# Wr loaded by GpSimd, product 7 by output tile, and B turned by VectorE instead of TensorE, in a two-layer fp32 kernel

## The reference

```python
# layer 0: dense W (1024x1024) plus a gated low-rank part, E=8 experts of rank R=16
base   = einsum('btd,od->bto', x, W)
logits = einsum('btd,ed->bte', x, Wr) + 5.0 * one_hot(language_id)      # Wr: 8x1024
topw, topi = top_k(logits, 2);  gates = one-hot sum of softmax(topw)
h      = einsum('btd,erd->bter', x, A)                                  # A: 8x16x1024
x = x + base + 2.0 * einsum('bter,bte,eor->bto', h, gates, B)           # B: 8x1024x16
# layer 1: one of 16 weight matrices for each batch row
x = x + einsum('bsi,boi->bso', x, w1[adapter_id])
```

## Time and profile before

| | |
|---|---|
| median of 3 runs | 396.96 us (396.77 to 397.57) |
| profiled execution | 396.9 us, of which 395.1 us are the span from the first to the last instruction |
| granted TensorE clock | 1.00 over the span (2.4 GHz, the upper of its two levels) |
| PE (TensorE matmul) busy | 389.8 us, 99% |
| DVE (VectorE) busy | 307.9 us, 78% |
| ACT (ScalarE) busy | 173.8 us, 44% |
| POOL (GpSimd) busy | 60.7 us, 15% |
| read and written in HBM | 53.51 MB and 14.68 MB |

### The profile page before, as it was taken

The page is one execution under the profiler, slowest core; times in us unless marked ns, Lnnn a source line. Parts: engine busy times, 40 slices in busy tenths (PEclk is TensorE's granted clock), DMA queues, the critical chain, the costliest instruction groups (busy, mean ns, idle before and its releaser), DMA issues.

```text
span 395.1 us, 5948 instructions
## 1 busy us (share of the span) xinstructions
PE 389.8 (99%) x1888; PEld 329.9 (83%) x1888; DVE 307.9 (78%) x415; ACT 173.8 (44%) x245; POOL 60.7 (15%) x86
## 2 busy tenths in 40 slices
PE   8999999999999999999999999999999999999996
PEld 8888988888889888888888888888888888888886
DVE  3899998988554757048877967999999999999600
ACT  3362283554400243254275334555665656556411
POOL 3134300000000000000110211332321231312000
PEclk9999999999999999999999999999999999999999
DMA  7999750113776100009492999999999999897212
GB/s 202 226 224 216 109 147 2 53 55 107 234 217 165 25 1 0 2 1 247 130 330 71 274 265 273 274 253 278 259 280 291 286 267 302 256 268 166 80 53 55
DMA packets 88129, 68.60 MB, mean 174 GB/s; under 512 B 16386, under 2 KB 87074, under 8 KB 87586
## 3 DMA queue, kind: packets, MB, share of 16 engines
q1 hardware_dynamic: 61472, 46.59, 49.2%
q10 hardware_dynamic: 26626, 21.64, 17.9%
HBM read 53.51 MB, written 14.68 MB: 173 GB/s over the span
## 4 chain that ended last, share of the span: by engine, by line
PE 97%; DMA 1%; SPq 1%; issue 0%; DVE 0%; ACT 0%
PE banks L1421 15%; PE banks L1419 15%; PE banks L1420 15%; PE banks L1282 13%; PE banks L1284 13%; PE banks L1283 13%; PE banks L1275 6%; PE banks L1260 2%; PE banks L1296 2%; PE banks L1293 2%; PE banks L1295 2%; DMA sums<-in_L_cond_Wr_dram 1%; PE banks L1314 0%; SPq L436 0%; SPq L483 0%; SPq L429 0%
## 5 line engine op out<-in xcount | busy, mean ns | idle before, releaser
L1282 PE MATMUL banks<-ring,weights 128*128 128x512 f32 x192 | 75.2, 392 | 0.0
L1420 PE MATMUL banks<-weights,tokens 128*128 128x512 f32 (+1 forms) x184 | 69.9, 380 | 0.0
L1421 PE MATMUL banks<-weights,tokens 128*128 128x512 f32 (+1 forms) x184 | 69.9, 380 | 0.0
L1419 PE MATMUL banks<-weights,tokens 128*128 128x512 f32 (+1 forms) x184 | 69.9, 380 | 0.0
L1106 ACT ACTIVATE weights<-weights_f 128x1024 fp32r<-128x1024 f32 x44 | 46.6, 1061 | 50.1 <-DVE weights_f L759 49.3
L512 POOL TENSOR_TENSOR raw<-raw,ident 128x128 f32<-128x128 f32 x42 | 30.0, 714 | 219.2 <-DMA raw<-in_L_cond_weight_dram 219.1
L759 DVE STREAM_TRANSPOSE weights_f<-raw 128x1024 f32<-128x1024 f32 x42 | 51.7, 1232 | 8.2 <-POOL raw L512 7.7
L765 DVE TENSOR_TENSOR weights<-weights_f,weights 128x1024 fp32r<-128x1024 f32 x44 | 52.7, 1198 | 0.7 <-ACT weights L1106 0.6
L1284 PE MATMUL banks<-ring,turned_w 128*128 128x512 f32 x128 | 49.8, 389 | 0.0
L1283 PE MATMUL banks<-tokens,weights 128*128 128x512 f32 x128 | 49.8, 389 | 0.0
L1282 PEld LDWEIGHTS banks<-ring,weights 128*128 128x128 f32 x192 | 36.0, 188 | 7.6 <-issue 0.3
(11 more groups left out here) (131 smaller groups left out, 626.0 us busy)
## 6 DMA issues: line engine op xcount, KB each, us to landing
raw<-in_L_cond_weight_dram SPq DMA_DIRECT2D x168, 128.0 KB, 5.2
ring_f<-in_L_cond_weight_dram SPq DMA_DIRECT2D x88, 128.0 KB, 5.5
out_dram<-sums ACTq DMA_DIRECT2D x31, 256.0 KB, 5.6
raw<-in_x_dram SPq DMA_DIRECT2D x48, 128.0 KB, 3.3
x_kept<-stage ACTq DMA_DIRECT2D x24, 256.0 KB, 3.1
raw<-in_L_cond_W_dram SPq DMA_DIRECT2D x16, 128.0 KB, 3.4
turned_w_f<-in_x_dram SPq DMA_DIRECT2D x12, 128.0 KB, 3.4
ring_f<-in_L_cond_W_dram SPq DMA_DIRECT2D x12, 128.0 KB, 3.6
```

The costliest lines, as they stand in the source:

```text
L1282: nc.tensor.matmul(ps, u_hi, x_hi, start=first and k == 0, stop=False, skip_group_check=True)
L1419: nc.tensor.matmul(ps, x_hi, w_hi, start=m == 0, stop=False)
L1420: nc.tensor.matmul(ps, x_hi, w_lo, start=False, stop=False)
L1421: mm = nc.tensor.matmul(ps, x_lo, w_hi, start=False, stop=m == M - 1)
```

## The change

1. **Front.** The four loads of Wr move from SP to GpSimd, behind the making of the identity. SP goes on from A's first half to W. A's second half moves behind the first two second halves of x, for SP and VectorE. On VectorE the low part `("wr", 0)` moves ahead of the turn of x's tile (0, 1, 0), and the bias work moves a little.
2. **Product 7 of span 0** is taken by output tile. TensorE waits for each tile's low weights and copied accumulator separately. The gated h is turned before tile 3 (36 matmuls of the product are done then, as before). Tile 3's s4, low weights and accumulator copy move behind the gates.
3. **B** is loaded so that a 32x32 block turn is all that it needs. VectorE turns it in one instruction between product 7's x parts and the gates. The 8 transposes of TensorE and the 4 copies of ScalarE go.

```diff
     def by_tile(s, i):
-        return s == 0 and i in (1, 2, 6, 5)
+        return s == 0 and i in (1, 2, 6, 7, 5)
...
@@ SyncE
             fill_a_half(sp, 0, (0, 1))
-            sp.wait_ge(wr_zeroed, 1)
-            for c in range(Q):
-                sp.dma_start(wr_raw[c * S:c * S + E, :], wr[:, c * DQ:(c + 1) * DQ]).then_inc(wr_loaded, 16)
             fill_w_half(sp, 0)
             for r in range(1, HM):
                 fill(sp, W0_PLACES[r], w0_rows(r), w_loaded[r])
+            fill_x(sp, 0, 1)
             fill_a_half(sp, 1)
-            fill_x(sp, 0, 1)
             fill_x(sp, 1, 1)
...
@@ GpSimd
+            pool.wait_ge(wr_zeroed, 1)
+            for c in range(Q):
+                pool.dma_start(wr_raw[c * S:c * S + E, :], wr[:, c * DQ:(c + 1) * DQ]).then_inc(wr_loaded, 16)
             pool.wait_ge(consts, 3)
...
@@ VectorE, the front
-            turn_half(("ah", 1))
             low(("wl", 3))
             turn_half(("xh", 0, 1))
             turn_half(("xh", 1, 1))
             low(("xr", 0))
             low(("xr", 1))
+            turn_half(("ah", 1))
             turn_half(("xh", 2, 1))
             turn_half(("xh", 3, 1))
             low(("xr", 2))
+            turn_half(("wh", 0, 1))
+            low(("xr", 3))
...
+            low(("wr", 0))
+            turn(x_item(0, 1, 0))
...
-            turn_half(("wh", 0, 1))
-            turn(x_item(0, 1, 0))
-            low(("wr", 0))
...
@@ VectorE, product 7 to the gates
-            for r in range(HM):
+            for r in range(HM - 1):
                 make_s4(r)
-            lows("u", 7)
+                low(("u", 7, r))
             lows("x", 0, 7)
+            dve.wait_ge(b_loaded, E * 16)
+            nc.vector.transpose(b_whole.rearrange("p (m q s) -> p q m s", m=M, q=Q),
+                                raw_tile(SLOT["b",]).rearrange("p (q m j) -> p q m j", q=Q, m=M)).then_inc(b_turned, 1)
             make_gates(0)
+            make_s4(HM - 1)
+            low(("u", 7, HM - 1))
             low(("b",))
             make_s1(0)
             low(("x", 0, 5, 0))
...
@@ TensorE
-                    if r == 1:
-                        turn_b()
+
+            def product_7():
+                for r in range(HM):
+                    if r == HM - 1:
+                        turn_gated(0)
+                    pe.wait_ge(lo_done, LOW_AT["u", 7, r] + 1)
+                    pe.wait_ge(u2_copied, r + 1)
+                    for k in range(HM):
+                        if r == 0:
+                            pe.wait_ge(lo_done, LOW_AT["x", 0, 7, k] + 1)
+                        step(0, 7, k, r, main_bank(0, r), False)
```

More of the change, by code:

```diff
@@ L75, in cond_resid_kernel @@
     FRONT = ([("xh", t, 0) for t in range(XT)] + [("ah", 0), ("wh", 0, 0)] + [("w", r) for r in range(1, HM)] +
-             [("ah", 1)] + [("xh", t, 1) for t in range(XT)] + [("wh", 0, 1)])
+             [("xh", 0, 1), ("xh", 1, 1), ("ah", 1), ("xh", 2, 1), ("xh", 3, 1), ("wh", 0, 1)])
     LOADS = ([x_item(0, 1, t) for t in range(XT)] + [("w", m) for m in range(HM, M)] + [("b",)] +
@@ L101, in cond_resid_kernel @@
     PIECES += [("x", 0, 6, t) for t in range(XT)] + [("u", 6, r) for r in range(HM)]
-    PIECES += [("u", 7, r) for r in range(HM)] + [("x", 0, 7, k) for k in range(HM)] + [("b",)]
+    PIECES += [("u", 7, r) for r in range(HM - 1)] + [("x", 0, 7, k) for k in range(HM)] + [("u", 7, HM - 1), ("b",)]
     PIECES += [("x", 0, 5, 0), ("u", 5, 0)] + [("x", 0, 5, k) for k in range(1, HM)] + [("u", 5, r) for r in range(1, HM)]
@@ L128, in cond_resid_kernel @@
     w1_rows = w1.rearrange("n o i -> (n o) i")
-    b_rows = b.rearrange("e (p j) r -> e p j r", p=P)
+    b_rows = b.rearrange("e (n s) r -> e s n r", s=S)
     x1_kept = nc.dram_tensor("x1_kept", [NB, P, M, T], F32, kind="Internal").ap()
@@ L279, in gT_ps @@
             return banks[:, at:at + 2, :]
-        def b_ps():
-            return banks[:, 4:6, :]
         def kept_slot(e):
@@ L326, in cond_resid_kernel @@
         b_turned = sem("b_turned")
-        b_copied = sem("b_copied")
         hi_done = sem("hi_done")
@@ L460, in load @@
                     for e in range(E):
-                        sp.dma_start(raw_tile(slot).rearrange("p (j e r) -> p e j r", j=M, e=E)[:, e],
+                        sp.dma_start(raw_tile(slot)[e // 2 * S:(e // 2 + 1) * S, :]
+                                     .rearrange("p (n i r) -> p i n r", i=2, r=R)[:, e % 2],
                                      b_rows[e]).then_inc(b_loaded, 16)
@@ L800, in _ @@
                                     lang_f[:].unsqueeze(2).to_broadcast([P, NB, E]), ALU.is_equal).then_inc(setup, 1)
-            low(("xr", 3))
+            low(("wr", 0))
+            turn(x_item(0, 1, 0))
             dve.wait_ge(setup, 3)
             nc.vector.tensor_scalar(bias[:], bias[:], LANG_BIAS, None, ALU.mult).then_inc(setup, 1)
-            turn_half(("wh", 0, 1))
-            turn(x_item(0, 1, 0))
-            low(("wr", 0))
             turn(x_item(0, 1, 1))
@@ L966, in high @@
                 elif kind == "b":
-                    act.wait_ge(b_copied, Q)
+                    act.wait_ge(b_turned, 1)
                 elif kind == "bd":
@@ L1153, in _ @@
             copy_h(0, 1)
-            highs("u", 7)
-            act.wait_ge(b_turned, 1)
-            for q in range(Q):
-                nc.scalar.activation(b_whole.rearrange("p (m q h j) -> p q m h j", m=M, q=Q, h=4)[:, q],
-                                     b_ps().rearrange("p a f -> p (a f)")
-                                     .rearrange("p (j q m h) -> p q m h j", j=M, q=Q, m=M)[:, q],
-                                     ACT.Copy).then_inc(b_copied, 1)
+            for r in range(HM - 1):
+                high(("u", 7, r))
             for r in range(HM - 1):
@@ L1163, in _ @@
             highs("x", 0, 7)
-            copy_u2(0, 3)
+            high(("u", 7, HM - 1))
             high(("b",))
@@ L1167, in _ @@
             high(("x", 0, 5, 0))
+            copy_u2(0, HM - 1)
             gT_high(0)
@@ L1297, in lora @@
                                  skip_group_check=True).then_inc(lora_done, 1)
-            def turn_b():
-                pe.wait_ge(b_loaded, E * 16)
-                pe.wait_ge(h_copied, 2)
-                flat = raw_tile(SLOT["b",])
-                for j in range(M):
-                    turn_j = nc.tensor.transpose(b_ps()[:, j // HM, (j % HM) * P:(j % HM + 1) * P],
-                                                 flat[:, j * P:(j + 1) * P], ident[:])
-                turn_j.then_inc(b_turned, 1)
             def turn_gated(s):
@@ L1310, in turn_gated @@
                 pe.wait_ge(p1_added, DRAINED * (s + 1))
-                if s == 0:
-                    pe.wait_ge(b_copied, Q)
                 for j in range(GT):
@@ L1366, in span @@
                     product(s, 6, lambda r: pe.wait_ge(p1_copied, HM * s + r + 1), False, main_bank)
-                gated = 2 if s else 3
-                product(s, 7, lambda r: pe.wait_ge(u2_copied, HM * s + r + 1), False, main_bank, range(gated))
-                turn_gated(s)
-                product(s, 7, None, False, main_bank, range(gated, HM))
+                    product(s, 7, lambda r: pe.wait_ge(u2_copied, HM * s + r + 1), False, main_bank, range(HM // 2))
+                    turn_gated(s)
+                    product(s, 7, None, False, main_bank, range(HM // 2, HM))
+                else:
+                    product_7()
                 pe.wait_ge(gT_done, s + 1)
```

## The result

The changed kernel takes 397.63 us (median of 22 runs) against 396.86 us for the kernel before (22 runs). The ratio is 1.0026, 95% interval 1.0013 to 1.0038. It is **slower by 1.0 us** by this ratio (0.5 to 1.5); the two medians are 0.77 apart. The forecast was no change, 396.8.

The account below looks back on a forecast made before the run. Bound: the features' start plus TensorE's own instructions and an output tail, with VectorE level at tile 1's drain. TensorE gains 0.40 and 0.88, but VectorE lets the drain move only -0.13: 396.9 - 0.13 = 396.8 us, range 396.4 to 397.1.

Parts of the forecast that it names:

- The front's gain at the features: Start of the feature matmuls: Wr lands before 9.7, features start at 10.15 instead of 10.55, TensorE gains 0.40 us.
- the bounds: GpSimd's issue of Wr's four loads at the front: between 1.38 us (SP's pace) and 3.81 us (three GpSimd instructions).
- The steps from the first s4 on: VectorE from product 6 to `gT_low`: measured step lengths added up, first s4 at 52.5, `gT_low` able to start at 69.24.
- The wait for tile 3's copy: TensorE ahead of `gT_low`: it loses about 0.3 us waiting for the copy of tile 3.
- 10.55 - 0.4 = 10.13: Front: the end of TensorE's warm-up matmuls, before which the features could not start.
- Rival (b): Front: GpSimd's issues are drawn out, Wr lands at 11.05, features start at 11.55; 398.2 us, chance 0.13.
- rival (c): Middle: VectorE's chain has unseen cover, so TensorE keeps its whole gain of 1.43 us; 395.5 us, chance 0.11.
- Rival (a): Front: the features' start does not move, or W's half keeps VectorE back; costs 0.27, 397.2 us, chance 0.16.
- The step that failed: VectorE from product 1 to 52.90: without idle time, it comes 0.4 to 0.5 us earlier, with TensorE.
- the sum's last term: VectorE's drain of tile 1, near 75.4: it moves as `gT_low` does, 69.24 - 69.37 = -0.13 us.
- Cost: nothing: Front: VectorE's pause where A's second half was turned, and SP's x loads held about 7 us longer, cost no time.
- The prediction's own pace: VectorE's chain before the gates: from 52.5 six instructions to 56.1, first low part at 56.9, fourth at 58.7.

Follow-up runs that it names:

- Experiment 3: Kernel before with only the four Wr loads moved from SP to GpSimd: 396.97 us, ratio 1.0001.
- experiment 4: Changed kernel with VectorE making the three s4 first, then product 7's three low weights, not in turn: 397.18 us, ratio 1.0002 to the kernel before.
- Experiment 8: Kernel before with one more VectorE instruction (0.72 us) ahead of the first s4: 397.37 us, ratio 1.0012.
- 0: The changed kernel again, unedited, against the kernel before: 397.70 us, ratio 1.0025.
- experiment 1: Kernel before with only the front of the change (Wr's loads on GpSimd, new orders on SP and VectorE): 396.73 us, ratio 0.9994.
- 6: Kernel before with only product 7 taken by output tile; B still turned by TensorE and copied by ScalarE: 397.60 us, ratio 1.0013.
- experiment 7: Kernel before with only B turned by VectorE, between product 7's low x parts and the gates: 396.65 us, ratio 0.9988.
- 9: Changed kernel with one more VectorE instruction (0.72 us) ahead of the first s4: 398.31 us, ratio 1.0039 to the kernel before.
- 10: Changed kernel with product 7 by part as before; front and B's turn on VectorE kept: 396.86 us, ratio 0.9999 to the kernel before.
- 11: Changed kernel with tile 3's s4 and weights ahead of the x parts again, product 7 still by tile: 397.48 us, ratio 1.0011 to the kernel before.
- 2: Kernel before with only the middle of the change (product 7 by tile, B turned by VectorE), front as before: 397.32 us, ratio 1.0013.
- the 401.6: A profiled execution of the unedited changed kernel, one of four of its 22 runs 1.4 us or more above the median: 401.6 us.

## Why the prediction was wrong

**What held.** The front's gain at the features (0.52 measured, 0.40 forecast) with Wr landed by 9.57, ahead of 9.7; GpSimd's issues took 2.23, between the bounds. The Trainium skill ("DMA: Bandwidth & Descriptors", Anatomy of one DMA — SWDGE (gpsimd) path) gives 2.0 us plus bytes by 436 GB/s for one. The trace disagrees here: four of 8 KB landed with a median of 5.0 us after their issue, while other loads kept the DMA engines full, and they overlapped, so the 8.1 us estimated from the page for four in a row did not come either. The 5.0 also answers the reason that the prediction gave for the slow Wr loads, "the x and A data ahead of them in SP's own queue": in GpSimd's own queue they took nearly as long as the 5.33 before. What came earlier was their issue, at 1.90 instead of 3.63.

The steps from the first s4 on held as well: turn of B + 1.16, gates + 5.2, tile 3 and the rest up to `gT_low` + 3.5, no idle left there. From the first s4 to `gT_low` the prediction has 16.7 and the trace 16.64. The wait for tile 3's copy was put at 0.3 and is 0.2. (The prediction's "10.55 - 0.4 = 10.13" holds with the wait of 0.42 before rounding.) Rival (b) fell with Wr's landing and rival (c) with the waits of TensorE. Rival (a) has the nearest time (397.2) but not the mechanism: the start did move.

**The step that failed**: "From there on VectorE's chain of turns and low parts has no idle time worth naming up to 52.90. It is tied to TensorE's product 2 near 32 us by a drain, so it comes some 0.4 to 0.5 earlier, with TensorE." VectorE was busy for 33.05 of the 34 us from 18 to 52 before, and for 31.44 after. That is 1.61 more idle, and it turned a lead of 0.86 (18.07 against 18.93 for the fourth addition to W's diagonal) into a lag of 0.75. I had read "no idle" as room to move. It was a balance: the loads arrived just in time for VectorE's old times. With it falls the sum's last term: the drain of tile 1, put at -0.13, moved by +0.86 in this execution, of which 0.75 is the first s4.

Why they do not arrive earlier: the rate at which the data came in hardly rose. The windows of 4 us in the kernel before and in the changed one (columns as above; DMA share and GB/s stand last):

```profile
16.00:20.00 4.00, 4.00 (x19) 3.29 (x18) 3.92 (x8) 2.25 (x5) 1.30 (x1) 1.00 0.90 215
20.00:24.00 4.00, 4.00 (x19) 3.30 (x19) 3.89 (x7) 3.21 (x7) 1.99 (x2) 1.00 0.88 218
```

```profile
16.00:20.00 4.00, 4.00 (x20) 3.30 (x19) 2.93 (x6) 2.78 (x6) 1.49 (x2) 1.00 1.24 221
20.00:24.00 4.00, 4.00 (x19) 3.34 (x18) 3.22 (x5) 2.25 (x5) 1.99 (x2) 1.00 1.17 227
```

SyncE issues at least 1.4 earlier, and the rate stays near 220 GB/s; over 4 to 28 us it is 230 GB/s in both. The requests only wait longer. The median from issue to landing of x's second halves grew from 3.4 to 5.8 us (first fence: before, second: changed):

```profile
turned_w_f<-in_x_dram SPq DMA_DIRECT2D x8, 128.0 KB, 3.4
```

```profile
turned_w_f<-in_x_dram SPq DMA_DIRECT2D x8, 128.0 KB, 5.8
```

Experiment 3 had the same with Wr's loads as its only edit (5.5). The thirteen profiles fall in two groups: 5.1 to 5.8 in the eight where GpSimd issues Wr, 3.2 to 3.9 in the five where SyncE does, at 225 to 237 GB/s over 4 to 28 us in all. A second, smaller part is "Cost: nothing" for the pause of 0.70 where A's second half had been turned. It is in every kernel with the changed front. In experiment 4, without late loads, the first s4 stood at 52.55 in spite of it, so the pause by itself was covered, as said. With late loads behind it the cover was gone.

**The second mis-sized point** is the cost of lateness. The third copy on ScalarE waits for the third s4, the high x parts stand behind it in ScalarE's queue, and VectorE pays 0.63. The prediction's own pace has this wait (VectorE done at 56.1, first low part at 56.9) and took it as free, since product 6 on TensorE would set the same time. That holds only with the first s4 at 52.5. With a late one VectorE alone sets it. Experiment 4 takes the alternation away and is 0.2% better by the points. TensorE's own gains, 0.52 from the start and 0.88 from B, then stand in its waits: 1.0 at the first x part of product 7, 0.2 at tile 3 and 0.3 at `gT_low`. Experiment 8's profile shows that the path through VectorE was nearly binding in the kernel before too. I had looked for its cover at the drain of tile 1 and at `gT_low`, and it was decided at product 7's first x part. In the eight profiles where TensorE waited there (0, 1, 6, 7, 8, 9, 10, 11), product 7's first weight load starts 0.73 to 0.81 behind the start of the low x parts. In the kernel before the low x parts start at 57.96 and the weight load, which waits for nothing, stands at

```profile
58.85 0.19 PEld L1282 LDWEIGHTS banks<-ring,weights 128*128 128x128 f32 x1
```

That is 0.89 behind, so the slack is 0.1 to 0.2 us.

**What is shown and what is not.** Shown: the middle alone costs 0.13% [0.04%, 0.22%]; the new list from the first s4 takes 0.6 us more than the old one where VectorE is the path (22.76 or 22.77 in five profiles against 22.16 to 22.25 in five), though against the kernel before itself, with 22.66, it is 0.1; what moved the first s4 came before 31 us, and in five of six profiles with the changed front it was the landing of one load; the front alone gives nothing that can be measured. Open: whether the front adds to the middle's loss (0.25% together against 0.13%, intervals that overlap). The mean first s4 of the profiles (53.04 and 52.95) says hardly, and the medians of the runs say a few tenths. With 53.04 and 22.77 the drain stands at 75.8, 0.25 behind the profile of before; the rest of the measured loss is not accounted for. It also remains open how far A's late landing belongs to the change: no experiment changed it alone. Taking the late loads away was not tried; the argument rests on executions in which they happened to be on time (4 and 7) or late (0, 2, 3, 10).

No combination beat the kernel before beyond its interval. The nearest is experiment 7, -0.12%.

## What to carry to other kernels

An engine that is busy without a gap need not be free to run earlier. Before you carry a gain through it, look at when its loads land, and at the DMA share there: where the rate is the limit, an earlier issue only makes a longer landing. And when work moves from the engine that looks busiest to one that looks free, find the first place where the first waits for the second. The slack at that place, 0.1 to 0.2 us here, is what the move can use, and not the 22% of idle time on the page.

## What the runs showed that I had not expected

- After 2.12 us without work TensorE's granted clock was 0.50 from 13 to 16 us, 1.5 us after it had started again at 11.47; after pauses of 0.2 to 1.1 us at that place (experiments 0, 2 and 9) it was 1.00 in that stretch.
- TensorE's warm-up does not end at a fixed time. It ended 0.4 before 10.55 in the profile of before, and at 9.36 in experiment 1, whose features then started at 9.48. I had used 10.13 as a floor for the start. The granted clock reads 1.00 throughout from 3 us, yet the pace of the warm-up matmuls changes within it: 6 to 8 start in each microsecond up to 8 us in the profile of before and 12 in the next; in experiment 2 it is 11 from 5 us on.
- In three profiles (the 401.6, experiments 4 and 10) TensorE stood for 1.4 to 2.8 us ahead of a matmul at 264 to 265 us, in layer 1, with no releaser shown. No run looks into it.
- The same program, up to the first s4, reached it at 53.65 and at 52.55 (experiments 0 and 4), with 1.48 and 0 us of waits for loads. One profile of a kernel is one draw from this.
